# Delta-rule block: the transposed inverse multiplies masked products and keys, in two visits of two pairs

## The reference

```
q, k = l2norm(xn @ Wq), l2norm(xn @ Wk);  v = silu(xn @ Wv);  beta = sigmoid(xn @ Wb)     # 16 heads of 32
S_t = S_{t-1} + k_t (beta_t (v_t - S_{t-1}^T k_t))^T ;   o_t = S_t^T q_t                  # delta rule, by head
out = x + (rmsnorm(o) * w) @ Wo + (silu(xn @ G * gs) * (xn @ U * us)) @ Dn * ds           # G, U, Dn rounded to fp8
```

## Time and profile before

| | us |
|---|---|
| median of 3 runs | 2215.24 |
| the profiled execution, its own time | 2216.21 |
| its span (first to last instruction) | 2214.5 |
| TensorE busy | 2112.6 (95%) |
| VectorE busy | 1862.5 (84%) |
| ScalarE busy | 1189.1 (54%) |
| GpSimd busy | 285.4 (13%) |
| mean granted TensorE clock | 0.992 |

### The profile page before, as it was taken

How to read it: one execution, slowest core, us unless ns; L and a number is a source line. 1 busy time by engine, 2 the same in 40 slices (tenths; PEclk the granted TensorE clock), 3 DMA queues, 4 the chain that set the end, 5 groups by cost and what they waited for, 6 DMA issues and landing times.

```text
span 2214.5 us, 87086 instructions
## 1 busy us (share of the span) xinstructions
PE 2112.6 (95%) x36976; PEld 1079.5 (49%) x36976; DVE 1862.5 (84%) x3348; ACT 1189.1 (54%) x3080; POOL 285.4 (13%) x534
## 2 busy tenths in 40 slices
PE   2789999999999999999999999999999999999996
PEld 1345454554545555454554545455454554545453
DVE  8887978889798887979888797888979888797886
ACT  4774545636456464645646455463645647455542
POOL 2101111021110201011020110201111020111100
PEclk9899999999999999999999999999999999999998
DMA  7001110001111011111001111001111001111000
GB/s 271 2 21 22 39 23 31 20 14 40 22 40 22 3 40 22 39 23 40 13 13 40 22 40 23 12 31 22 40 22 40 17 8 40 22 40 22 15 9 20
DMA packets 89971, 68.77 MB, mean 31 GB/s; under 512 B 68480, under 2 KB 68480, under 8 KB 89600
## 3 DMA queue, kind: packets, MB, share of 16 engines
q1 hardware_dynamic: 88880, 63.20, 10.4%
q10 hardware_dynamic: 720, 0.03, 0.0%
HBM read 30.72 MB, written 16.78 MB: 21 GB/s over the span
## 4 chain that ended last, share of the span: by engine, by line
PE 85%; DVE 7%; ACT 4%; issue 2%; DMA 1%; SPq 0%; ACTq 0%
PE D L478 27%; PE D L458 22%; PE D L547 13%; PE T L383 12%; PE D L399 8%; PE T L375 4%; DVE state L1412 2%; ACT kpv L781 1%; ACT at L807 1%; ACT f_hi L768 1%; DVE outer_p L1408 1%; DVE kpv L1397 1%; DMA qt<-in_L_attn_Wq_dram 1%; DVE outer_v L1298 0%; DVE at L1305 0%
## 5 line engine op out<-in xcount | busy, mean ns | idle before, releaser
L478 PE MATMUL D<-xt,wgu 128*128 128x512 f16 x3072 | 687.0, 381 | 9.1 <-issue 7.9
L458 PE MATMUL D<-xt,w_hi 128*128 128x512 f16 x1536 | 461.7, 383 | 23.9 <-DVE w_lo L1075 23.9
L478 PEld LDWEIGHTS D<-xt,wgu 128*128 128x128 f16 x3072 | 293.0, 98 | 360.3 <-issue 13.5
L458 PE MATMUL D<-xt,w_lo 128*128 128x512 f16 x768 | 293.5, 382 | 0.0
L547 PE MATMUL D<-wd,f_lo 128*128 128x512 bf16 x768 | 292.7, 381 | 0.0
L547 PE MATMUL D<-wd,f_hi 128*128 128x512 bf16 x768 | 292.2, 381 | 0.0
L863 ACT ACTIVATE qt<-T 64x128 f32<-64x128 f32 (+1 forms) x384 | 104.7, 273 | 348.5 <-DVE outer_p L1408 345.5
L1298 DVE TENSOR_TENSOR outer_v<-mt,at 128x62 f32<-128x62 f32 (+15 forms) x496 | 259.5, 523 | 13.6
L1305 DVE TENSOR_TENSOR at<-at,outer_v 128x62 f32<-128x62 f32 (+15 forms) x496 | 260.4, 525 | 11.8
L764 ACT ACTIVATE kpv<-kpv,rk 128x32 f32<-128x32 f32 x1024 | 231.2, 308 | 33.8 <-DVE kpv L1167 33.8
L458 PEld LDWEIGHTS D<-xt,w_hi 128*128 128x128 f16 x1536 | 145.6, 98 | 196.8 <-issue 28.8
(11 more groups left out here) (182 smaller groups left out, 2928.3 us busy)
## 6 DMA issues: line engine op xcount, KB each, us to landing
xs<-_attn_hidden_states_dram SPq DMA_DIRECT2D x32, 512.0 KB, 3.6
out_dram<-xs SPq DMA_DIRECT2D x32, 512.0 KB, 2.8
fuse<-in_L_ffn_gate_w_dram SPq DMA_DIRECT2D x2, 768.0 KB, 8.4
xs<-in_L_ffn_up_w_dram SPq DMA_DIRECT2D x2, 768.0 KB, 9.0
f_hi<-in_L_ffn_down_w_dram SPq DMA_DIRECT2D x2, 768.0 KB, 10.6
f_lo<-in_L_ffn_down_w_dram SPq DMA_DIRECT2D x2, 768.0 KB, 12.2
kpv<-in_L_attn_Wk_dram SPq DMA_DIRECT2D x1, 1024.0 KB, 11.2
qt<-in_L_attn_Wq_dram SPq DMA_DIRECT2D x1, 1024.0 KB, 13.4
```

The source lines that it names most:

```text
L458: last = nc.tensor.matmul(D[bank][:, :], w[:, k, cols], xp[:, k, :], start=n == 0, stop=n == len(products) - 1)
L478: last = nc.tensor.matmul(D[bank][:, :], wgu[:, n // 2, c:c + P], (xt_hi, xt_lo)[n % 2][:, n // 2, :], start=n == 0, stop=n == 2 * KT_ - 1)
```

## The change

1. `t_transposed` reads T by columns instead of rows (a stride of 32 elements in the innermost dimension), so `tt` holds what makes the matmul multiply by the transposed inverse.
2. The product visits take `kpv[:, 0:2]` (masked products p and keys k) instead of keys and values. The results T^T p and T^T k replace p and k in place. The chain subtracts the state's part from v itself, and its r visit multiplies the difference by those results. `read_w` is gone: the transposed keys that are in `kq` anyway are used.
3. ScalarE copies both halves of each bank (`copy_products`: 2x256 columns instead of 256), with no wait for VectorE.
4. TensorE makes two product visits in a row (m = 0, 1 and m = 2, 3), with twenty dense matmuls behind each two. The first chain visit waits for 6 banks copied, the r visit of c = 0 for all 8.
5. On ScalarE, `norm_rows(0)` and `(1)` stand ahead of the copies, and the copies stand four banks at a time; `high_part(9)` and `(10)` and `silu_gate(11)` stand behind them. On VectorE, `low_part(9)` stands ahead of the chain instead of inside chunk 0, and `low_part(10)` moves from chunk 1 to chunk 0.
6. In the opening turn `beta_tanh` moves behind `evacuate_q(2)`.

```
 for m in range(MS):                                        # TensorE
     pe.wait_ge(tt_ready, since(2, m // 2 + 1))
     ...
-            pe.wait_ge(u_ready, since(8, 2 * m - 2))
+            pe.wait_ge(pk_ready, since(8, 2 * m - 2))
     ...
-                             kpv[:, 1:3, pc * DH:(pc + 1) * DH], b == 1)
+                             kpv[:, 0:2, pc * DH:(pc + 1) * DH], b == 1)
     last.then_inc(tiled_done, 2)
-    fill(fill_uw(m), FILL_UW)
+    if m % 2:
+        fill(fill_uw(m - 1), 2 * FILL_UW)
 for c in range(STEPS):
-    if c == 0:
-        pe.wait_ge(w_ready, since(8, 8))
     pe.wait_ge(s_ready, since(STEPS, c))
-    pe.wait_ge(*((o_ready, since(STEPS, c - 1)) if c >= 2 else (u_ready, since(8, 8))))
+    pe.wait_ge(*((o_ready, since(STEPS, c - 1)) if c >= 2 else (pk_ready, since(8, 6 + 2 * c))))
     ...
+    if c == 0:
+        pe.wait_ge(pk_ready, since(8, 8))
     pe.wait_ge(r_ready, since(STEPS, c + 1))

-def copy_u(g):                                             # ScalarE
-    act.wait_ge(w_ready, since(8, g + 1))
-    made = T[g % 4][:, :].rearrange("p (n a d) -> p n a d", n=8, a=2)
+def copy_products(g):
+    act.wait_ge(tiled_done, since(TILED, DONE_UW + g + 1))
+    made = T[g % 4][:, :].rearrange("p (n a d) -> p a n d", n=8, a=2)
     for to, src in parts_of(g % 2):
-        last = nc.scalar.activation(vt[to, 8 * g:8 * g + 8, :], made[src, :, 1, :], ACT.Copy)
-    last.then_inc(u_ready, 1)
+        last = nc.scalar.activation(kpv[to, 0:2, 8 * g * DH:8 * (g + 1) * DH].rearrange("p a (n d) -> p a n d", n=8),
+                                    made[src], ACT.Copy)
+    last.then_inc(pk_ready, 1)

-nc.vector.transpose(tt[:, s], t_prob[:, s])                # VectorE
+nc.vector.transpose(tt[:, s], t_prob[:, s].rearrange("p i c -> p c i"))
```

More of the change, by code:

```diff
@@ L215, in delta_block_kernel @@
         q_sqs = [fuse[:, 2, :], fuse[:, 3, :], sg[:, 0, :], sg[:, 1, :]]
-        u_v = vt[:, :, :].rearrange("p (m b c) d -> p b c m d", m=MS, b=BATCH)
+        r_v = vt[:, :, :].rearrange("p (m b c) d -> p b c m d", m=MS, b=BATCH)
         ot_v = qt[:, :, :].rearrange("p (m b c) t -> p b c m t", m=MS, b=BATCH)
@@ L270, in delta_block_kernel @@
         tt_ready, p_ready = sem("tt_ready"), sem("p_ready")
-        u_ready, w_ready, r_ready, s_ready = sem("u_ready"), sem("w_ready"), sem("r_ready"), sem("s_ready")
+        pk_ready, r_ready, s_ready = sem("pk_ready"), sem("r_ready"), sem("s_ready")
         ws_read, ds_read = sem("ws_read"), sem("ds_read")
@@ L569, in all_spans @@
                     pe.wait_ge(kt_ready, since(MS, MS))
-                    pe.wait_ge(vk_ready, since(1, 1))
                     for m in range(MS):
@@ L728, in all_spans @@
                         magnitude_of(GU_PIECES + 1)
-                        beta_tanh()
                         square_of(2)
@@ L734, in all_spans @@
                         evacuate_q(2)
+                        beta_tanh()
                         square_of(5)
@@ L830, in all_spans @@
                     scaled.then_inc(vk_ready, 1)
-                    copy_u(0)
-                    copy_u(1)
+                    norm_rows(0)
+                    norm_rows(1)
+                    copy_products(0)
+                    copy_products(1)
+                    copy_products(2)
+                    copy_products(3)
                     silu_gate(9)
-                    norm_rows(0)
-                    copy_u(2)
-                    copy_u(3)
+                    high_part(8)
+                    norm_rows(2)
                     silu_gate(10)
[L838 to L841, removed]
+                    norm_rows(3)
+                    copy_products(4)
+                    copy_products(5)
+                    copy_products(6)
+                    copy_products(7)
                     high_part(9)
-                    norm_rows(2)
-                    copy_u(6)
-                    copy_u(7)
                     silu_gate(11)
-                    norm_rows(3)
+                    high_part(10)
                     if not opening:
@@ L853, in all_spans @@
                             square_q(SQUARE_AT[c])
-                        if c < 2:
-                            high_part(10 + c)
+                        if c == 1:
+                            high_part(11)
                         if c in HIGH_AT and not closing:
@@ L1314, in t_transposed @@
                         after(solved[0])
[L1315 to L1321, removed]
+                        nc.vector.transpose(tt[:, s], t_prob[:, s].rearrange("p i c -> p c i")).then_inc(tt_ready, 1)
                     def add_out(j):
@@ L1354, in all_spans @@
                     t_transposed(1)
-                    read_w(0)
                     low_part(0)
-                    read_w(1)
                     low_part(1)
                     low_part(2)
-                    read_w(2)
                     low_part(3)
-                    read_w(3)
                     fuse_tile(8)
@@ L1365, in all_spans @@
                     low_part(5)
-                    read_w(4)
                     low_part(6)
-                    read_w(5)
                     fuse_tile(9)
                     low_part(7)
-                    read_w(6)
                     low_part(8)
-                    read_w(7)
                     fuse_tile(10)
+                    low_part(9)
                     def read_down(j):
@@ L1393, in all_spans @@
                         if c == 0:
-                            dve.wait_ge(u_ready, since(8, 8))
+                            dve.wait_ge(vk_ready, since(1, 1))
                         dve.wait_ge(ws_read, since(STEPS, c + 1))
-                        u = u_v[:, :, c]
-                        nc.vector.tensor_tensor(u, u, blocks(outer_v), ALU.subtract).then_inc(r_ready, 1)
+                        r = r_v[:, :, c]
+                        nc.vector.tensor_tensor(r, r, blocks(outer_v), ALU.subtract).then_inc(r_ready, 1)
                         if c:
                             add_inner(c - 1)
-                        if c < 2:
-                            low_part(9 + c)
+                        if c == 0:
+                            low_part(10)
                         if c in DOWN_FIRST:
```

## The result

| | us |
|---|---|
| before, median of 4 runs (2213.98 to 2216.39) | 2214.72 |
| after, median of 4 runs (2316.34 to 2326.49) | 2323.39 |
| ratio, 95% interval | 1.0483 (1.0469 to 1.0497) |
| forecast | 2239 (2216 to 2256) |
| span of the profiled execution, before and after | 2214.5 and 2314.6 |

The sign was right and the size was not: +24 us forecast, +108.7 measured. The profiled execution is the quickest of the four runs after the change, so its trace explains 100 us of the 109.

The account below looks back on a forecast made before the run. TensorE, holding 85% of the chain, was taken as the bound. Fifteen turns at +1.56 (-1.15, +0.45, +0.43, +1.8), closing turn +0.4 and opening 0 made +23.8: 2239 us from the median, range 2216 to 2256 (8 in 10).

Parts of the forecast that it names:

- The sign: Whole kernel: forecast slower, 2239 us, with a chance of 0.84 for slower.
- the free-running TensorE: TensorE without new waits, product visits to r visit: joining two visits saves 0.23, r visit 1.15 us a turn earlier.
- The forecast of 15.56: TensorE in a middle turn: 15.56 us from the first product visit to the chain's first visit.
- the gate at the r visit: Chunk 0's r visit waits for VectorE's subtraction, behind low 9 and high 9: a new TensorE wait of 1.8 us a turn.
- the copies: ScalarE's 512-column copies out of PSUM: 0.605 us each, bounds 0.52 and 0.70, twelve a turn.
- the wait of the earlier trace gone: TensorE's wait of 0.69 us for ScalarE's copy at the chain's first visit disappears.
- silu 10 behind half 20: On ScalarE, silu 10 waits for half 20, whose last four matmuls stand behind m = 3; silu 10 at 1084.96.
- the waits of 0.45 and 0.43 at m = 2 and m = 3: TensorE's product visits m = 2 and 3 wait for copies held behind norm_rows and rstd: 0.45 and 0.43 us.
- The strided transpose: VectorE's two transposes of T: the stride costs 0 to 1.5 us in 1024 elements, taken as 0.
- The rival of the falling clock: TensorE's clock falls behind the 1.8 us idle at every r visit: +1.6 us x 15, 2263; chance 0.08.
- `beta_tanh` in the opening: Moving beta_tanh in the opening turn: effect taken as 0, with 3.75 as the bound below and +0.5 above.
- rivals that reorder the same waits: New waits covered, whole gain, 2197, chance 0.11; or norm_rows does not hold the copies, 2226, chance 0.13.

Follow-up runs that it names:

- e9: e8 with the product visits joined in pairs again and nothing else changed: 2282.98 us, ratio 1.0292.
- e8: Changed kernel with single product visits, ScalarE's copies of m = 0 ahead of norm_rows(0), high_part(9) early, VectorE's four subtractions broken up: 2211.14 us, ratio 0.9984.
- e3: Changed kernel with high_part(9) moved from behind the last copy to between norm_rows(2) and silu_gate(10): 2283.36 us, ratio 1.0309.
- e5: Changed kernel with TensorE's program padded so the product visits stand 64 instruction slots later within a block of 256: 2542.29 us, one run.
- e6: Changed kernel with five of the twenty dense matmuls put between the two visits of a pair: 2240.09 us, ratio 1.0121.
- e2: Kernel before with the pairing alone: product visits in pairs, twenty dense matmuls behind each pair: 2318.56 us, ratio 1.0464.
- e1: Changed kernel with the pairing taken out, ten dense matmuls behind each product visit again: 2229.29 us, ratio 1.0052.
- e7: e1 with high_part(9) moved early as in e3: 2223.32 us, ratio 1.0034.

## Why the prediction was wrong

- **The step that failed** is "the free-running TensorE": that joining two visits saves 0.31 + 0.15 - 0.216 - 0.01 = 0.23, because tiled work goes on after 0.01. It took the spacing of records inside one visit as one that holds through two. A pair was to last 2.92 from its start to the next dense matmul (1072.75 to 1075.67); measured were 4.85 and 4.66 (980.95 to 985.80, 990.22 to 994.88), 3.7 more for the two. The forecast of 15.56 held 0.9 of other waits, which these breaks replace, so turn 7 is only 2.8 above it (18.35). Longer breaks in other turns, and slower dense matmuls behind 11 of the 32, bring the mean to 4.4 above (20.00). That is 71 us in 16 turns. Taking the pairing out gives the same size, 70.0 (e9 against e8); that the two numbers lie so close is luck, since they count from different starting points. No bound was given for it, since the sum treated it as read from a row. It was not: no row of the kernel before shows 512 tiled instructions in a run.
- **There was a sign.** The code pads to `FETCH_SLOTS`, and the sum never asked what for. And single visits of the kernel before sometimes last longer than their 1.59, at the same work and the same clock, most often the last of a turn:

```profile
948.11 1.59 PE L383 MATMUL T<-kpv,mt 32*32 32x64 f32 x128
951.89 1.81 PE L383 MATMUL T<-kpv,mt 32*32 32x64 f32 x128
```

  In the second visit here it is the same limit, just touched. Its single records step by 0.01 us, but once, at record 56, by 0.14, and that step ends 1.46 us after the end of a packet of the instruction queue; the breaks of the changed kernel end 1.20 to 1.55 after one (below). A visit in the turn at 410.95 has such a step too, of 0.18. Most of the other long visits are only 0.05 to 0.1 longer, without one large step, and stay unexplained.
- **Right in mechanism and size:** the gate at the r visit (3.84 forecast, 3.77 the mean; removed by e3); the copies (0.605 forecast, 0.61 measured); the wait of the earlier trace rows gone; silu 10 behind half 20.
- **Not to be seen:** the waits of 0.45 and 0.43 at m = 2 and m = 3. The breaks in the pairs delay TensorE by more, and cover them. They were also forecast too long: `rstd` was done 3.59 us behind the first visit (980.95, 984.54), not 4.26, mostly because GpSimd's last two steps took 1.46 and 0.24 instead of 1.57 and 0.57. By the prediction's own walk that leaves no wait at m = 2 and some 0.2 at m = 3, an estimate. In turn 11 alone, where the power took 3.27, do they show: 0.71 and 0.25.
- **The strided transpose** costs 0.73 each, half way between the bounds of 0 and 1.5; taken as 0. It costs the turn 0.24, some 3.6 us in all. The direction that the Trainium skill, "SBUF — State Buffer" (under "Door 1"), gives for such a stride is what the trace shows.
- **The rival of the falling clock**, given 0.08 at every r visit, does occur, and it is part of the loss. Behind the r wait it shows in three turns, in which the stretch to the last r visit took 34.2 to 34.5 instead of 32.9 or less. Behind the breaks, which the prediction did not have, it shows in 11 of 32 stretches. Its price of 1.6 us was near that of the falls seen (1.52 for twenty dense matmuls in turn 4).
- **`beta_tanh` in the opening**, taken as 0: the first product visit starts at 144.12 against 144.77, and between 143.6 and 145.6 in the other runs with that move. No effect can be told.
- The range (2216 to 2256) was made from the prices of the copies and `rstd` and from rivals that reorder the same waits. All its bounds were of things already in the sum.

That a break is the end of a block of instructions not yet there rests on four findings: it moves with the program's position (e5), its distance is 510 instructions, it shortens when five dense matmuls give time (e6), and the trace shows the packet that it waits for. The page of the profile has the instruction queue at 305 packets for 5.00 MB, 16.4 KB each. The Trainium skill, "Runtime: NRT & Kernel Launch", section "Instruction fetch mechanics", describes blocks of 16 KiB, 256 instructions, read ahead in sequence; the size agrees. It also calls the cost of a boundary mostly hidden; of these visits the trace says otherwise. If the break is the end of a block, the end of the block before it lies 256 instructions or 128 records earlier, at record 88, 0.95 us into the pair; work resumed 3.3 us after that in the turn at 980.95, and 3.8 in the turn at 561.38. Windows of the first of these, from record 88 to the start of the packet, the packet, and from its end to the resumption (columns as above):

```profile
981.90:982.76 0.86, 0.86 (x94) 0.86 (x83) 0.86 (x2) 0.36 (x2) 0.27 (x2) 1.00 0.00 0
982.76:983.76 1.00, 0.84 (x77) 0.70 (x57) 1.00 (x2) 0.00 (x0) 1.00 (x1) 1.00 0.06 16
983.76:985.16 1.40, 0.00 (x0) 0.00 (x1) 1.40 (x4) 0.59 (x1) 0.63 (x2) 1.00 0.00 0
```

The 16 GB/s over 1.00 us are the one packet of 16384 bytes. All 32 breaks of the changed kernel look like this: the packet starts 0.74 to 1.59 us behind that record, takes 0.92 to 1.41, and TensorE resumes 1.20 to 1.55 after its end, 3.0 to 3.8 us together. In that time a pair wants 512 instructions and more, while a single visit and its ten dense matmuls need 276 in 3.78 (542.67 to 546.45). What sets the three parts was not tried: no run changed the fetch itself, or the other traffic while it went on.

## What to carry to other kernels

Count instructions per microsecond on the engine that bounds, not busy time alone: before joining two runs of small matmuls, find the longest such run that the trace shows without a break, and treat everything longer as unpriced, with a bound of its own. Dense matmuls between visits are not only work to hide latency; at 216 ns for a matmul and its weight load they are the time in which the next ones arrive. And when work moves to the end of an in-order engine's queue, look for the small step behind it (here high 9, 0.6 us) that another engine waits for: moving that one instruction took 28 us of waiting at the gate out of the trace, and 40 us off the median.

## What the runs showed of the chip that was not expected

- TensorE broke off inside visits wherever 512 tiled instructions came in about 2.8 us: 32 breaks in the changed kernel, 1.21 to 2.15 us each and 56.8 in all; 32 with 54.2 us in e2; 32 with 58.3 in e9. Each ended 1.2 to 1.6 us after the end of a packet of the instruction queue. Single visits of 256 followed by ten dense matmuls did not break so (at most 0.29).
- Behind breaks of 1.5 to 2.1 us the granted clock fell to 0.50 in some turns, and twenty dense matmuls took up to 6.28 us for 4.49; in others it stayed at 1.00 behind breaks just as long.
- GpSimd's power on 4 elements a row took 1.46 us or 3.28, beside the same VectorE subtractions, with starts that differ by 0.01 us: long in one turn of the changed kernel, three of e1, five of e7. Once the four subtractions were no longer back to back (e8, e9) the long form did not appear in 30 turns. Why it is one or the other in a given turn stays open.
- A block transpose of 1024 fp32 columns took 1.22 us from neighbouring elements and 1.95 from elements 32 apart.
